# Flamingo block on one core: the score weights of both batches made in the prologue, batch 1's output weights spread over three slots

## The reference

```
B, N, D = 2, 1024, 256          # 2 batches of 1024 rows of x
M = 77                          # context rows of each batch
# H, HD = 8, 64 heads; F = 1024 hidden
q = layernorm(x) @ Wq;  k = ctx @ Wk;  v = ctx @ Wv           # per head
attn = softmax(q k^T / 8) over the 77 context rows
x = x + tanh(g_xattn) * (attn v @ Wo + bo)
h = relu(fixed_quant(fixed_quant(layernorm(x)) @ w1q^T + b1q))   # 8-bit fixed point
x = x + tanh(g_ffn) * (h @ w2q^T + b2q)
```

## Time and profile before

| | us |
|---|---|
| median of 3 runs | 125.9 (125.42 to 126.14) |
| profiled execution, its own time | 125.8 |
| its span, first to last instruction | 123.8 |
| TensorE (PE) busy | 118.5, 96% |
| VectorE (DVE) busy | 98.2, 79% |
| POOL busy | 84.6, 68% |
| ScalarE (ACT) busy | 78.2, 63% |

### The profile page before, as it was taken

One profiled execution on the slowest core, in us unless ns is written; L12 is line 12 of the kernel. 1 busy time (PEld: TensorE's weight loads), 2 busy tenths in 40 slices (PEclk: granted clock), 3 DMA queues, 4 the chain that ended last, 5 costly groups with the idle time before them and its releaser, 6 DMA issues.

```text
span 123.8 us, 2908 instructions
## 1 busy us (share of the span) xinstructions
PE 118.5 (96%) x1029; PEld 107.4 (87%) x1029; DVE 98.2 (79%) x218; ACT 78.2 (63%) x167; POOL 84.6 (68%) x157
## 2 busy tenths in 40 slices
PE   7999999979999999999999999999999999999990
PEld 2689968969995999999999999999999997988780
DVE  3017999698999989989899999999797969447981
ACT  4155591999888484999384857566664728357520
POOL 3002229288794979698989958995899595987610
PEclk9999999999999999999999999999999999999999
DMA  2999699300000000000002000100200020020104
GB/s 68 338 266 334 227 380 382 139 5 0 3 0 8 0 0 3 0 0 5 0 0 85 5 0 36 48 5 3 83 1 0 5 87 0 0 80 10 54 30 169
DMA packets 5311, 8.86 MB, mean 72 GB/s; under 512 B 1175, under 2 KB 2226, under 8 KB 5170
## 3 DMA queue, kind: packets, MB, share of 16 engines
q1 hardware_dynamic: 5210, 8.61, 19.5%
q10 hardware_dynamic: 88, 0.08, 0.2%
HBM read 6.59 MB, written 2.10 MB: 70 GB/s over the span
## 4 chain that ended last, share of the span: by engine, by line
PE 86%; DVE 5%; ACT 3%; POOL 2%; issue 2%; DVEq 0%; POOLq 0%; ACTq 0%
PE sc_ps L741 21%; PE of_ps L774 20%; PE h_ps L801 9%; PE tr_ps L753 7%; PE of_ps L816 7%; PE tr_ps L686 4%; PE of_ps L679 3%; PE h_ps L708 3%; PE tr_ps L724 2%; PE h_ps L695 2%; PE tr_ps L816 1%; PE sc_ps L816 1%; POOL probs L266 1%; PE sc_ps L695 1%; PE of_ps L782 1%
## 5 line engine op out<-in xcount | busy, mean ns | idle before, releaser
L741 PE MATMUL sc_ps<-a_sb,xT 128*128 128x308 f32 x192 | 31.2, 311 | 0.0
L774 PE MATMUL of_ps<-u_sb,pT 128*128 128x256 f32 x240 | 30.6, 279 | 0.3 <-ACT x2T L414 0.2
L774 PEld LDWEIGHTS of_ps<-u_sb,pT 128*128 128x128 f32 x240 | 29.1, 188 | 1.2 <-issue 1.1
L741 PEld LDWEIGHTS sc_ps<-a_sb,xT 128*128 128x128 f32 x192 | 27.5, 189 | 0.7 <-issue 0.4
L382 ACT ACTIVATE probs<-probs,rstd 128x616 f32<-128x616 f32 x16 | 13.1, 817 | 23.1 <-DVE probs L543 23.0
L408 ACT ACTIVATE hid_q<-h_ps,b1z 128x256 int8<-128x256 f32 x58 | 24.8, 495 | 3.9 <-PE h_ps L801 3.9
L266 POOL TENSOR_TENSOR probs<-probs,rden 128x616 f32<-128x616 f32 x16 | 19.5, 1221 | 3.2 <-DVE rden L553 3.2
L311 POOL CAST hid<-hid_q 128x512 bf16<-128x512 int8 x27 | 15.8, 611 | 2.0 <-ACT hid_q L408 2.0
L801 PE MATMUL h_ps<-x2T,w1T 128*128 128x256 bf16 x128 | 16.6, 273 | 0.0
L538 DVE TENSOR_REDUCE mx<-sc_ps 128x8 f32<-128x616 f32 x16 | 12.7, 792 | 4.7 <-PE sc_ps L741 4.6
L394 ACT CAST pT<-tr_ps 128x640 fp32r<-128x640 f32 x16 | 11.1, 691 | 4.8 <-PE tr_ps L753 4.8
(11 more groups left out here) (103 smaller groups left out, 187.7 us busy)
## 6 DMA issues: line engine op xcount, KB each, us to landing
w_sb<-in_L_ffn_w_dram SPq DMA_DIRECT2D x2, 1024.0 KB, 10.9
out_dram<-x_sb SPq DMA_DIRECT2D x7, 256.0 KB, 2.5
x_sb<-in_x_dram SPq DMA_DIRECT2D x4, 256.0 KB, 8.6
x_sb<-in_x_dram SPq DMA_DIRECT2D x1, 1024.0 KB, 9.8
wk_sb<-in_L_xattn_Wk_dram SPq DMA_DIRECT2D x1, 512.0 KB, 3.8
wq_sb<-in_L_xattn_Wq_dram SPq DMA_DIRECT2D x1, 512.0 KB, 5.7
wv_sb<-in_L_xattn_Wv_dram SPq DMA_DIRECT2D x1, 512.0 KB, 8.3
wo_sb<-in_L_xattn_Wo_dram SPq DMA_DIRECT2D x1, 512.0 KB, 8.5
```

The source lines that it names most:

```text
L741: ins = nc.tensor.matmul(sc_ps[:, a, 0:HALF], xT[:, T % 2, p, c, :], a_sb[:, q, T // TB, c, HALF * a:HALF * a + HALF], start=first, stop=last)
L774: ins = nc.tensor.matmul(attn_ps, pT[:, T % 2, p, P * c:P * c + P], u_sb[:, q, MC * (T // TB) + c, :], start=first, stop=last)
```

## The change

The score weights of both batches are made together in the prologue: kT holds both batches side by side, and one product has 154 columns. Four units, (c, half) with half = two of the four pairs of heads, go to of_ps, sc_ps, tr_ps and h_ps. Each unit is copied out by two ScalarE instructions of 308 elements, one for each batch: batch 0's becomes the high part, batch 1's goes whole into the new tile a1_whole. VectorE makes batch 0's low parts in four subtractions. POOL makes batch 1's high and low parts from a1_whole (a1_parts), the first half in the prologue, the second in slot 0. The first two transposes of rows now go through of_ps bank 0, and the values' projections through of_ps bank 1 and tr_ps. Batch 1's U is made a bank at a time in slots 1, 2 and 3; the whole values of its first two pieces go to the new tile u1_whole, and POOL makes their low parts in slots 2 and 3. In slot 0 exponentials(1) and denominators(1) now come first, as in the other slots; in the prologue exponentials(0) comes ahead of xT_copy(2). What is left out below are the declarations of tiles and semaphores and the maps of banks.

```diff
@@ POOL
-            def a_low(c, n):
-                pool.wait_ge(copied, n)
-                nc.gpsimd.tensor_tensor(a_sb[:, 1, 1, c, :], full[:, :], a_sb[:, 0, 1, c, :].bitcast(F32),
-                                        ALU.subtract).then_inc(copied_low, 1)
+            def a1_parts(c):
+
+                pool.wait_ge(a1_copied, 3 + c)
+                nc.gpsimd.tensor_copy(a_sb[:, 0, 1, c, :], a1_whole[:, c, :]).then_inc(a1_high, 1)
+                pool.wait_ge(a1_high, c + 1)
+                nc.gpsimd.tensor_tensor(a_sb[:, 1, 1, c, :], a1_whole[:, c, :], a_sb[:, 0, 1, c, :].bitcast(F32),
+                                        ALU.subtract).then_inc(a1_low, 1)
             def u_low(n):
-                pool.wait_ge(copied, 3)
-                nc.gpsimd.tensor_tensor(u_of(1, n, 1), full[:, 0:2 * D], u_of(1, n, 0).bitcast(F32),
-                                        ALU.subtract).then_inc(copied_low, 1)
+                pool.wait_ge(u_high, 4 + n)
+                pool.wait_ge(u1_copied, n + 1)
+                nc.gpsimd.tensor_tensor(u_of(1, n, 1), u1_whole[:, n, :], u_of(1, n, 0).bitcast(F32),
+                                        ALU.subtract).then_inc(u1_low, 1)
...
             rstd_first(0, 2)
+            a1_parts(0)
             rstd_first(2, 4)
...
-                if s in (0, 1):
-                    a_low(s, s + 1)
+                if s == 0:
+                    a1_parts(1)
...
-                if s == 3:
-                    u_low(1)
+                if s in (2, 3):
+                    u_low(s - 2)
@@ ScalarE
-            def a_copy(b, c):
-                act.wait_ge(a_psum, DK * b + c + 1)
-                nc.scalar.copy(a_of(b, c, 0), a_banks[b, c]).then_inc(a_high, 1)
+            def a_copy(n):
+
+                c, half = a_units[n]
+                act.wait_ge(a_psum, n + 1)
+                nc.scalar.copy(a_part(a_sb[:, 0, 0, c, :], half), a_psum_of(c, half, 0)).then_inc(a_high, 1)
+
+            def a1_copy(n):
+
+                c, half = a_units[n]
+                act.wait_ge(a_psum, n + 1)
+
+                if half == 1:
+                    act.wait_ge(a_ready, n + 1)
+                nc.scalar.copy(a_part(a1_whole[:, c, :], half), a_psum_of(c, half, 1)).then_inc(a1_copied, 1)
+
+            def u1_copy(n):
+                act.wait_ge(u_psum, 4 + n)
+                nc.scalar.copy(u1_whole[:, n, :], u_banks[1, n]).then_inc(u1_copied, 1)
...
-            a_copy(0, 0)
-            a_copy(0, 1)
+            a_copy(0)
+            a1_copy(0)
+            a_copy(1)
+            a1_copy(1)
+            a_copy(2)
+            a_copy(3)
             act.wait_ge(xT_psum, 2)
             nc.scalar.copy(xT[:, :, 0, :, :].rearrange("p i c n -> p i (c n)"),
-                           h_ps[:, 0, :].rearrange("p (i n) -> p i n", i=2)).then_inc(xT_high, 2)
+                           of_ps[:, 0, :].rearrange("p (i n) -> p i n", i=2)).then_inc(xT_high, 2)
+            a1_copy(2)
+            a1_copy(3)
...
+            exponentials(0)
             xT_copy(2)
-            exponentials(0)
...
             for s in range(TILES):
-                if s == 0:
-                    pT_copy(0)
-                    xT_copy(3)
                 if live(s + 1):
                     exponentials(s + 1)
-                if s > 0:
-                    pT_copy(s)
-                if live(s + 3) and s > 0:
+                pT_copy(s)
+                if live(s + 3):
                     xT_copy(s + 3)
...
                 if s == 0:
-                    a_copy(1, 0)
-                    nc.scalar.copy(full[:, :].rearrange("p (a m) -> p a m", a=2), a_banks[1, 0]).then_inc(copied, 1)
                     round_weights(w1_in, w1_sb, w1q, w1_rounded)
                 if s == 1:
-                    a_copy(1, 1)
-                    act.wait_ge(copied_low, 1)
-                    nc.scalar.copy(full[:, :].rearrange("p (a m) -> p a m", a=2), a_banks[1, 1]).then_inc(copied, 1)
                     w1T_copy()
+                if s in (1, 2):
+                    u_copy(1, s - 1)
+                    u1_copy(s - 1)
                 if s == 3:
-                    u_copy(1, 0)
-                    u_copy(1, 1)
-                    act.wait_ge(copied_low, 2)
-                    nc.scalar.copy(full[:, 0:2 * D], u_banks[1, 1]).then_inc(copied, 1)
                     u_copy(1, 2)
@@ VectorE
-            def a_low(b, c):
-                dve.wait_ge(a_high, DK * b + c + 1)
-                nc.vector.tensor_tensor(a_of(b, c, 1), a_banks[b, c], a_of(b, c, 0).bitcast(F32), ALU.subtract).then_inc(a_ready, 1)
+            def a_low(n):
+                c, half = a_units[n]
+                dve.wait_ge(a_high, n + 1)
+                if half == 0:
+                    dve.wait_ge(a1_copied, n + 1)
+                nc.vector.tensor_tensor(a_part(a_sb[:, 1, 0, c, :], half), a_psum_of(c, half, 0),
+                                        a_part(a_sb[:, 0, 0, c, :], half).bitcast(F32), ALU.subtract).then_inc(a_ready, 1)
...
-                if live(s + 1) and s > 0:
+                if live(s + 1):
                     denominators(s + 1)
                 probsT_low(s)
                 if live(s + 3):
                     rowsT_low(s + 3)
-                if s == 0:
-                    denominators(1)
-                if s in (3, 4):
-                    u_low(1, 2 * (s - 3))
+                if s == 4:
+                    u_low(1, 2)
@@ TensorE
-            def score_weights(b, c, pairs):
-
-                for j in pairs:
+            def score_weights(c, half):
+
+                for j in range(2 * half, 2 * half + 2):
                     for q in range(2):
-                        rows = slice(HD * q, HD * q + HD)
-                        ins = nc.tensor.matmul(a_banks[b, c][:, q, M * j:M * j + M], wqT[rows, j, P * c:P * c + P],
-                                               kT[rows, j, M * b:M * b + M], start=True, stop=True, tile_position=(HD * q, 0))
-                if PAIRS - 1 in pairs:
-                    ins.then_inc(a_psum, 1)
+                        rows, at = slice(HD * q, HD * q + HD), MP * (j % 2)
+                        ins = nc.tensor.matmul(a_banks[c, half][:, q, at:at + MP], wqT[rows, j, P * c:P * c + P],
+                                               kT[rows, j, :], start=True, stop=True, tile_position=(HD * q, 0))
+                ins.then_inc(a_psum, 1)
...
                 for c in range(DK):
-                    score_weights(0, c, (2 * j, 2 * j + 1))
+                    score_weights(c, j)
+
+            pe.wait_ge(a_ready, 1)
+            pe.wait_ge(a1_copied, 1)
...
-            pe.wait_ge(a_high, 2)
-            pe.wait_ge(a_ready, 1)
+            pe.wait_ge(a_high, len(a_units))
+            pe.wait_ge(a_ready, 2)
+            pe.wait_ge(a1_copied, 2)
             scores(0)
-            pe.wait_ge(v01_ready, 2)
-            keysT(wv_sb, v_psum, (2, 3), 0)
+            pe.wait_ge(a1_copied, 3)
+            keysT(wv_sb, v_psum, (2, 3), v_banks[1])
             rowsT(2)
             pe.wait_ge(wo_in, 16)
-            output_weights(0)
+            pe.wait_ge(v01_ready, 2)
+            pe.wait_ge(a1_copied, 4)
+            output_weights(0, (0, 1, 2))
             scores(1)
 
             for s in range(TILES):
                 if live(s + 3):
                     rowsT(s + 3)
-                if s == 0:
-                    pe.wait_ge(u_ready, 2)
-                    score_weights(1, 0, range(PAIRS))
                 probsT(s)
                 if s == 1:
                     weights1T()
-                    pe.wait_ge(copied, 1)
-                    score_weights(1, 1, range(PAIRS))
                 if s == 3:
-                    pe.wait_ge(copied, 2)
                     pe.wait_ge(w1T_ready, 2)
-                    output_weights(1)
+                if s in (1, 2, 3):
+                    output_weights(1, (s - 1,))
```

More of the change, by code:

```diff
@@ L87, in flamingo_kernel @@
         u_sb = sb("u_sb", [P, 2, B * MC, D], F32R)
-        full = sb("full", [P, HM])
+        a1_whole = sb("a1_whole", [P, DK, HM])
+        u1_whole = sb("u1_whole", [P, 2, 2 * D])
         w1q = sb("w1q", [P, FC, D], I8)
@@ L152, in probs_v, with a_psum_of, a_part @@
             return probs[:, T % 2, :].rearrange("p (h m) -> p h m", m=MW)[:, :, HEAD0:HEAD0 + M]
+        v_banks = of_ps[:, 1, 0:2 * MP], tr_ps[:, 0:2 * MP]
         def pair_bank(j, q):
-            return tr_ps[HD * q:HD * q + HD, 512 * j:512 * j + 2 * MP].rearrange("p (c b m) -> p c b m", c=2, b=B)
-        a_banks = {(0, 0): sc_ps[:, :, 0:HALF], (0, 1): of_ps[:, :, 0:HALF],
-                   (1, 0): h_ps[:, :, 0:HALF], (1, 1): h_ps[:, :, 0:HALF]}
-        def a_of(b, c, part):
-            return a_sb[:, part, b, c, :].rearrange("p (a m) -> p a m", a=2)
+            return v_banks[j][HD * q:HD * q + HD, :].rearrange("p (c b m) -> p c b m", c=2, b=B)
+        a_banks = {(0, 0): of_ps, (1, 0): sc_ps, (0, 1): tr_banks, (1, 1): h_ps}
+        def a_psum_of(c, half, b):
```

(29 more changed lines are left out.)

27 lines of the change are left out of this document (13 added, 14 removed).

## The result

The changed kernel takes 124.32 us (median of 4 runs, 124.16 to 124.37); the kernel before takes 125.75 in the runs beside it. The ratio is 0.988, with a 95% interval of 0.985 to 0.991: 1.2% faster, 1.4 us. The forecast was 124.1, its range 123.3 to 125.4.

What follows compares the result with a forecast made beforehand. Latency sets the prologue and slot 0, TensorE slots 1 to 13. The terms -0.6 - 1.05 - 0.1 = -1.75 us (+0.31 and +0.46 inside the -0.6) take the median from 125.9 to 124.1 us, range 123.3 to 125.4.

Steps and rivals of the forecast that it cites:

- Step 1: Prologue: 32 score-weight instructions with 154 instead of 77 columns take 2.10 against 1.79 us, +0.31 us on TensorE's path.
- rival C: Prologue score weights: the two row halves go one after the other, 126.1 us, no change; chance 0.07.
- rival B: Prologue score weights: a half's next load waits for that half's stream, 0.7 us more, 124.8 us; chance 0.08.
- Step 2: Prologue: eight ScalarE copies at 0.40 us each are just hidden, as are VectorE's subtractions and POOL's new parts.
- rival D: Prologue: the eight copies set its length, deciding from 0.62 us a copy; at 0.83 the time is 127.5; chance 0.08.
- Step 3: Prologue: exponentials(0) ahead of xT_copy(2) makes den(0) 0.65 us later, and center(1) ends 0.46 us later.
- Step 4: Slot 0: TensorE's wait for POOL goes and probsT(1) starts at 25.8 instead of 26.39 us, -0.6 us.
- Step 5: Slots 1 to 3: score weights leave and output weights are spread, net -1.05 us; attend(3) gives another -0.1.
- cover (a): Slots 1 to 3: VectorE's 5.10 us a slot against TensorE's 5.5, 5.5 and 5.1 to 5.3; it catches up later.
- cover (b): Slots 1 to 3: ScalarE's moved copies fit; rounding w2 ends near 37.2 us and exp(4), at 37.59 before, starts there.
- each slot as long as before: From slot 4 on: the chain is on TensorE alone and slot lengths do not change; no term in the sum.
- Rival A: Slots 2 to 5 become as short as VectorE's work and POOL's chain; two scales 0.4 late give 124.9 us; chance 0.16.

Runs made afterwards that it cites:

- fill: Changed kernel with the first piece of batch 1's U made in slot 0, between probsT(0) and scores(2), instead of slot 1: 124.48 us.
- U in slot 3: Changed kernel with all of batch 1's U made in slot 3 again, its copies and subtractions too: ratio 1.0015 to the kernel before.

## Why the prediction was right, point by point

**Step 1, score weights, +0.31.** Right. From the start of the score weights to scores(0) it is 3.78 us for 3.49: +0.29, in nine of the ten profiles of that order. The bounds' far end (+2.4, rival C) and rival B did not come. The Trainium skill's rule of step 1 ("TensorE: Matmul & The Clock Gate", "What overlaps and what doesn't") would, reckoned as in rival B, give a unit 0.71 us, and a unit takes 0.53, so the trace does not bear it out here either. The prediction's reading that the granted clock is 1.00 throughout went too far: the record of before begins at 5.88 us, and the first instructions of the first projection ran at half pace. No term of the sum rests on them.

**Step 2, the copies.** Right in kind, too dear: 416 to 462 ns each, but 0.31 to 0.35 from start to start, where 0.40 was reckoned; rival D is out. From the start of the score weights, xT's copy ended after 3.90 us (12.38 - 8.48) and in the repeated run after 3.64, for a forecast of 3.76. What I missed is another chain: the first transposes now write the bank of unit 0, so they wait for VectorE's first subtraction, which is queued behind VectorE's centring of x's first tiles. In the profiled execution these landed late (VectorE starts on them at 9.10 us, at 8.45 to 8.69 in five others), and 0.25 us went there (4.04 for 3.78).

**Step 3, the swap, +0.46.** Right, and near in size, but most of it is not the swap's. The 0.46 holds step 1's 0.31; what is left for the swap is some 0.2, and center(1), held by scores(1) almost as long, shows 0.1: it starts 7.57 us behind scores(0), 7.45 in the kernel before and 7.45 with the swap undone. Den(0) starts 5.48 behind scores(0), forecast 5.36.

**Step 4, slot 0, -0.6.** Right. probsT(1) starts 13.08 us behind scores(0) for 13.96, and with the +0.29 of step 1 that is -0.59. The bare starts (25.60 for 26.39) say -0.8 only because they take in what differs ahead of the score weights. The wait ahead of scores(2), VectorE as its releaser, and none ahead of probsT(1) came as forecast; it is 0.7 us by TensorE's row. Two edits share this gain and do not add: from scores(0) to probsT(1), the new order alone brings 0.95 us in the kernel before, and 0.75 are there without it in the changed kernel, for 0.88 with both.

**Step 5, slots 1 to 3, -1.05 and -0.1.** Too much by 0.2: from probsT(1) to slot 4 it is 16.42 us for 17.37, -0.95 for -1.15. Sixteen output-weight instructions take 1.00 us there and not 0.93, in slot 1 and again in slot 2, and attend(3) keeps its 1.96. That slot 4 begins at 42.02, forecast near 42, is luck: this shortfall and the 0.25 of step 2 are made up by the 0.46 us by which this execution began its score weights earlier, its clock having risen at 4.71 us for 5.88. And the reason was told too lightly. TensorE's work is the bound there only because U is spread: with it left in slot 3 the waits ate the same 1.5 us. I had listed VectorE's cover (a) as thin and it held. Of ScalarE's cover (b) I checked the exponentials and not rowsT_second, which had no slack at all in slot 2: TensorE work taken away ahead of it, as in fill, gains nothing unless ScalarE comes to it earlier too.

**After slot 4: "each slot as long as before".** Wrong, by 0.46 us (80.5 for 80.05). 0.3 of it is the pace of attend's products, 117 for 114 ns, set by where the tiles behind the new ones lie. The term in the sum was nought, without a thought given to it; no row of before could have shown it. The other 0.16 is attend(4)'s wait for rowsT_second(2), cover (b) once more, one slot behind those that were checked. It is there in every kernel built on the change but U in slot 3: attend(4) starts 1.96 to 2.08 us behind scores(6), 1.81 in the kernel before.

**The sum.** The number came out better than its terms. From the start of the score weights to the end, the steps give -0.59 - 0.95 + 0.46, some -1.1 us (113.8 for 114.9), where -1.75 was forecast; 125.9 less 1.1 would be 124.8, still inside the range. The medians differ by 1.4 to 1.6. 0.2 of that lies outside the span: the execution's time is 1.8 us longer than the span in every kernel built on the change and 2.0 in the kernel before and the two built on it. The rest lies ahead of the score weights, where the kernels do not differ. Neither is explained, neither was forecast, and both helped.

Rival A did not come in the changed kernel as VectorE's or POOL's. What came in a small way is its like in ScalarE, attend(4)'s 0.16 us, and the fill shows how near more of it was.

## What to carry to other kernels

Work taken off the bounding engine pays only as far as the next engine's length of the same slot: spread what is left so that no slot falls below it, and fill a gap only after asking what every other queue then has to deliver earlier. When a gain vanishes, look for the one instruction that the waiting engine needs and for what merely stands ahead of it in its queue. Compare kernels from a fixed point in the program to the end, since what differs between executions ahead of it can hide half a per cent, and declare new tiles last, or check that no unrelated product has changed its pace.

## What was not expected of the hardware

- The pace of fp32r products of 256 columns follows the SBUF addresses of pT and the tiles beside it: 114, 117 or 119 ns for three placings of the tiles behind u_sb, the first two shown in both kernels. Scores' products did not change (149 to 151 ns each from slot 6 on, in both kernels).
- Sixteen instructions of the first projection take 2.34 or 4.42 us in different executions of one kernel. The granted clock rose at 4.71 us in the one and at 9.78 in the other, behind the same work; the projection's instructions leave every 255 to 259 ns ahead of the rise and every 130 to 135 behind it. A clock row that prints 1.00 from the start can hide this.
- A load and product of 56 ns with 77 columns cost 65 with 154: twice the columns for 17% more time.
- Attend follows the ScalarE copy that frees its bank by 0.14 to 0.15 us wherever it is held by it, so a gap of that size between the two is a wait and not slack.
- Kernels built on the change spend 1.8 us outside the span, the others 2.0. Not explained.
